# Two more matmuls with unread results in each of the first eight steps of a batch's heads

## The chip, the cores and the metric

The kernel runs on one core of one Trainium2 chip. The metric is the device time of one execution in microseconds (us). Before the change three runs took 1752.15, 1747.69 and 1748.93 us, a median of 1748.93 us.

## What is computed

The reference is a chain of four blocks over 4 sequences of 1024 tokens with 256 features, each followed by a residual and a layer norm: a gated convolution with an MLP, a mixture of 32 experts, an attention with 16 heads, and a gated MLP whose hidden values are thinned to 2 of 4. The change lies in the attention:

```python
q = (x @ w_q.T).reshape(Bc, Tc, H, D).transpose(0, 2, 1, 3)
k = (x @ w_k.T).reshape(Bc, Tc, H, D).transpose(0, 2, 1, 3)
v = (x @ w_v.T).reshape(Bc, Tc, H, D).transpose(0, 2, 1, 3)
q = _rope(q)
k = _rope(k)
scores = jnp.einsum('bhqd,bhkd->bhqk', q, k) * SCALE
scores = jnp.where(tok_mask[None, None], scores, -jnp.inf)
attn = jax.nn.softmax(scores, axis=-1)
ctx = jnp.einsum('bhqk,bhkd->bhqd', attn, v)
```

Every query sees its own and all earlier blocks of 64 keys (the mask is causal by block), and the softmax is taken over each row.

## The kernel before, in words

There are three phases (convolution and MLP; experts; attention and last MLP), each with one instruction list per engine, written out by hand: the order of a list is the order of the code, and semaphores alone tie the engines together. The third phase, `attention_ffn_phase`, takes the four sequences one after the other ("batches", b = 0 to 3). A batch has its heads first, then the output projection, the MLP and its residual; pieces of the next batch's projections are woven into the MLP.

The 16 heads of a batch are four groups (g = 0 to 3) of four heads, each two pairs. The softmax needs the maximum of every row before the exponentials, so every score is computed twice on TensorE:

- `for_maximum(b, g, m)` (L1938 and L1941) makes a piece of plain scores for maximum m of group g, 40 maxima to a group. VectorE reads the piece and reduces it (`maximum`, L1681 and L1686). The pieces go round three PSUM banks; for_maximum waits on `mx_ok` until VectorE has read the piece that lay in the bank before.
- `scores(b, g, s)` (L1965) makes the transposed scores of step s, 20 steps (`STEPS`) to a group, with the maximum already folded into q. They go into one of two double banks, `W[s % 2]`, after ScalarE's exponentials of step s - 2 have read it (`exp_ok`). ScalarE takes the exponentials (`exponentials`, L1522).
- `weighted(b, g, u, part)` (L1985), once for two steps, multiplies the weights with v, in float32, four heads beside each other in the array.
- `sums_transposed` (L1995) turns the sums back, and VectorE divides (`normalised`).

In `heads(b)` on TensorE, each step s issues the maxima due in it (`max_jobs`), then `scores` of step s + 1, then, in even steps, `weighted` of the two steps before. The maxima are made ahead: group 0's own maxima are made in the batch before (or at the phase's start), and in group 0 the first eight steps (`AHEAD` = 8) make three maxima each for group 1; all later steps make two. VectorE and ScalarE walk through the same steps.

`kept_busy(bank, count)` (L2001) exists already: it issues `count` matmuls of a 128x128 identity (float16) with 512 columns of `w_qk`, whose results nobody reads. Before the change it is called once per batch, with six matmuls, behind `scores(b, 0, 0)`, ahead of the transposes of q with its maximum (`q_max_transposed`, L1917), which ScalarE copies (L1516) before `scores(b, 0, 1)` can start.

Of the kernel before, what the change touches and what calls it, by code (L numbers as in the profile page):

```python
# [62 lines left out]
def wait(eng, sem, value):  # L63

    if not isinstance(value, int) or value > 0:
        eng.wait_ge(sem, value)  # L66
# [1053 lines left out]
LEAD = 4  # L1120
# [15 lines left out]
STEPS = 2 * NU  # L1136
AHEAD = 8
# [20 lines left out]
def attention_ffn_phase(nc, io, keep):  # L1158
    with ExitStack() as ctx:  # L1159
# [67 lines left out]
        W = S[0:2]  # L1227
# [56 lines left out]
        def group(b, g):  # L1284

            return Step(None, 0, b * NHG + g)
# [5 lines left out]
        def max_jobs(g, s):  # L1292

            if g == 0 and s < AHEAD:
                return ((1, 3 * s, 3 * s + 3),)
            low = AHEAD + 2 * s
            return ((g + 1, low, low + 2),) if low < 2 * NX else ((g + 2, low - 2 * NX, low - 2 * NX + 2),)
# [595 lines left out]
        def _(pe):  # L1893
# [20 lines left out]
            def q_max_transposed(b, pair):  # L1914
                wait(pe, nm_ok, group(b, 0)(2, LEAD + pair + 1))
                for t in range(ST):
                    last = pe.transpose(q_max_bank(pair)[:, t * P:(t + 1) * P], rows_of(0, 0, pair)[:, t * P:(t + 1) * P], ident_h[:, :])  # L1917
                last.then_inc(tm_mm, 1)

            def for_maximum(b, g, m):  # L1920
                pair, k = divmod(m, NX)
                head = 64 * (k % 2)
                q = group(b, g)
                if k == 0:
                    wait(pe, qk_in[pair], q(32, 32))
                if (g, m) == (0, 0):
                    wait(pe, qkv_ok, (b + 1) * ST)
                if g == 0:
                    wait(pe, mx_ok, q(2 * NX, LEAD + m - 1))
                else:  # L1930
                    wait(pe, *ring_bank_read(b, turns["max", g, m]))
                bank = max_bank(g, m)
                query, key = of_pair(qT, g, pair), of_pair(kT, g, pair)
                at = 0
                for i, j, count in PIECES[k // 2]:
                    plain = count - (j + count - 1 == i)
                    if plain:
                        last = pe.matmul(bank[:, at * P:(at + plain) * P], query[head:head + NORM, i * P:(i + 1) * P],  # L1938
                                         key[head:head + NORM, j * P:(j + plain) * P], start=True, stop=True)
                    if plain < count:  # L1940
                        last = pe.matmul(bank[:, (at + plain) * P:(at + count) * P],  # L1941
                                         query[head:head + USED, i * P:(i + 1) * P],
                                         key[head:head + USED, i * P:(i + 1) * P], start=True, stop=True)
                    at += count
                last.then_inc(x_mm, 1)

            def for_maxima(b, g, low, high):
                for m in range(low, high):
                    for_maximum(b, g, m)

            def scores(b, g, s):
                u, pair = divmod(s, 2)
                q = group(b, g)
                if u == 0:
                    q_max_landed(pe, b, g, pair)
                wait(pe, exp_ok, q(STEPS, LEAD + s - 1))
                query, key = of_pair(qT, g, pair), of_pair(kT, g, pair)
                at = 0
                for j, i, count in UNITS[u][1]:
                    for rows, low, high in ((USED, i, i + 1), (FILTER, i + 1, i + count)) if i == j else (  # L1960
                            (FILTER, i, i + count),):
                        if high > low:
                            for head in range(2):
                                first = 64 * head
                                last = pe.matmul(W[s % 2][:, head, (at + low - i) * P:(at + high - i) * P],  # L1965
                                                 key[first:first + rows, j * P:(j + 1) * P],
                                                 query[first:first + rows, low * P:high * P], start=True, stop=True)
                    at += count
                last.then_inc(sc_mm, 1)

            def weighted(b, g, u, part):
                half = UNITS[u][0]
                q = group(b, g)
                first = u in (0, ENDS[0] + 1)
                if part == 0:
                    wait(pe, exp_ok, q(STEPS, LEAD + 2 * u + 2))
                    if first:
                        wait(pe, ev_ok, q(2, LEAD + half))
                    if (g, u) == (0, 0):
                        wait(pe, f2_ok, 2 * b)  # L1980
                if part == len(WEIGHTED[u]):
                    return
                at, j, i, count = WEIGHTED[u][part]
                for h in range(HG):
                    last = pe.matmul(O[32 * h:32 * h + 32, (i - half * GT) * P:(i - half * GT + count) * P],  # L1985
                                     v[:, j, g * HG + h, :], weights[(g * NU + u) % SLOTS_P][:, h, at * P:(at + count) * P],
                                     start=first and part == 0, stop=u in ENDS)
                if part == len(WEIGHTED[u]) - 1:
                    last.then_inc(pv_mm, 1)

            def sums_transposed(b, g, half):
                wait(pe, ev_ok, group(b, g)(2, LEAD + half + 1))
                wait(pe, *ring_bank_read(b, turns["sum", g, half]))
                for t in range(GT):
                    last = pe.transpose(sum_bank(g, half)[:, t * P:(t + 1) * P], oT[half][:, t * P:(t + 1) * P], ident[:])  # L1995
                last.then_inc(bt_mm, 1)

            def kept_busy(bank, count):

                for i in range(count):  # L2000
                    pe.matmul(bank, ident_h[:, :], w_qk[:, 0, 0, :], start=True, stop=True)  # L2001

            def heads(b):
                scores(b, 0, 0)
                kept_busy(S[1][:, 0, :], 6)
                q_max_transposed(b, 1)
                for g in range(NHG):
                    for s in range(STEPS):
                        if s == 0 and g > 0:
                            weighted(b, g - 1, NU - 1, 0)  # L2010
                        for of, low, high in max_jobs(g, s):
                            if of < NHG:
                                for_maxima(b, of, low, high)
                        if s + 1 < STEPS:
                            scores(b, g, s + 1)
                        elif g + 1 < NHG:
                            scores(b, g + 1, 0)
                        if s == 1 and g > 0:
                            sums_transposed(b, g - 1, 1)
                        if s == 9:  # L2020
                            sums_transposed(b, g, 0)
                        if s > 0 and s % 2 == 0:
                            weighted(b, g, s // 2 - 1, 0)
                        if s > 0 and s % 2 == 0:
                            weighted(b, g, s // 2 - 1, 1)
                weighted(b, NHG - 1, NU - 1, 0)
                sums_transposed(b, NHG - 1, 1)
# [69 lines left out]
            for b in range(NB):  # L2097
# [13 lines left out]
                def at_end_of_second(t, i):  # L2111
                    if ahead and t > 0:
                        for_maximum(c, 0, 28 + 4 * (t - 1) + i)

                heads(b)
                if b == 0:
                    pe.wait_ge(consts, 16 * 5)
# [111 lines left out]
```

## Time and profile before

| | before |
|---|---|
| median of three runs | 1748.93 us |
| profiled execution, its own time | 1751.17 us |
| its span, first to last instruction | 1749.4 us |
| mean granted TensorE clock | 0.914 of full speed |
| TensorE matmul busy | 1486.2 us (85%) |
| VectorE busy | 1140.8 us (65%) |
| ScalarE busy | 732.8 us (42%) |

Busy times overlap, since the engines run beside each other. A matmul's end is modelled with its latency, so a TensorE shown as busy may still be waiting between matmuls; the granted clock is the share of full speed at which the array ran, and in a stretch of uniform clock it reads 1.00 (2.4 GHz) or 0.50 (1.2 GHz).

### The profile page before, as it was taken

The page shows a single profiled execution, that of the slowest core. Times are in us where ns is not written, and L with a number is a line of the kernel's source. Part 1 is how long each engine was busy: PE and PEld are TensorE (multiplying, and loading weights), DVE is VectorE, ACT ScalarE, POOL GpSimd, SP SyncE. Part 2 cuts the span into 40 slices and gives each one's busy share as a digit, 9 for nine tenths or more (in the row PEclk, how much of TensorE's full clock was granted, in tenths as well). Part 3 has the DMA queues.
Part 4 walks back from the last instruction along what each step waited for, and adds up shares of the span by engine and source line. Part 5 has one row for each costly group of instructions (what it writes and reads, how often), then busy time and mean ns, then how long its engine had stood idle before and what let it go on. Part 6 is the DMA issues. An engine that isn't in the chain of part 4 may idle for free.

```text
span 1749.4 us, 25732 instructions
## 1 busy us (share of the span) xinstructions
PE 1486.2 (85%) x9682; PEld 827.5 (47%) x9683; DVE 1140.8 (65%) x2275; ACT 732.8 (42%) x1232; POOL 244.8 (14%) x249
## 2 busy tenths in 40 slices
PE   4999999877989983589878988878998788988796
PEld 2666666653657873223343533253533254433355
DVE  5666666636421135678669779768779678688475
ACT  5444455512212220426744137843137752157530
POOL 3344444411410001000020000120000120000000
PEclk8999999978999977758999979998979998989999
DMA  2000001005105512222101022101022101221000
GB/s 111 13 25 25 24 26 33 24 13 180 36 24 148 157 38 105 42 37 43 31 16 34 1 43 55 37 19 31 6 38 56 43 19 25 37 34 34 31 1 25
DMA packets 137483, 75.21 MB, mean 43 GB/s; under 512 B 117648, under 2 KB 126352, under 8 KB 136592
## 3 DMA queue, kind: packets, MB, share of 16 engines
q1 hardware_dynamic: 136800, 72.02, 16.6%
q0 software_dynamic: 576, 1.77, 0.4%
q8 instruction: 67, 1.10, 0.3%
q14 instruction: 40, 0.33, 0.1%
HBM read 37.59 MB, written 9.06 MB: 27 GB/s over the span
## 4 chain that ended last, share of the span: by engine, by line
issue 58%; POOL 3%; DVE 0%; POOLq 0%; DVEq 0%
POOL xs_sb L1448 1%; POOL rs_sb L1442 1%; POOL ve_sb L1439 0%; POOL qks_sb L1462 0%; POOL v_sb L1460 0%; DVE bn_sb L1620 0%; POOL qks_sb L1452 0%; DVE x_sb_sb L1635 0%; POOLq L1159 0%; POOLq L66 0%; DVE mv_sb L1626 0%; DVEq L1159 0%; POOL v_sb L1459 0%; POOL qks_sb L1463 0%; DVE ident_h_sb L1808 0%
## 5 line engine op out<-in xcount | busy, mean ns | idle before, releaser
L1522 ACT ACTIVATE room_sb<-s_ps 128x1024 f32<-128x1024 f32 (+1 forms) x320 | 291.2, 941 | 173.7 <-PE s_ps L1965 169.8
L1686 DVE TENSOR_REDUCE mx_sb<-s_ps 128x1 f32<-128x512 f32 (+1 forms) x400 | 249.6, 650 | 73.1 <-PE s_ps L1941 46.8
L1938 PE MATMUL s_ps<-room_sb 48*128 48x512 f16 (+3 forms) x480 | 155.9, 362 | 30.2 <-DVE mx_sb L1681 17.1
L1985 PE MATMUL cm_ps<-room_sb,v_sb 128*32 128x512 f32 (+3 forms) x1536 | 171.3, 536 | 0.8 <-ACT room_sb L1528 0.8
L1965 PE MATMUL s_ps<-room_sb 51*128 51x128 f16 (+4 forms) x1152 | 154.1, 288 | 15.4 <-ACT room_sb L1522 10.6
L2080 PE MATMUL cm_ps<-w_fd_sb,room_sb 128*128 128x256 f32 x512 | 132.7, 408 | 13.3 <-DVE room_sb L1764 13.3
L1439 POOL TENSOR_TENSOR ve_sb<-mv_sb,eps_sb 128x4 f32<-128x4 f32 x24 | 5.0, 210 | 951.2 <-DVE mv_sb L1626 951.2
L396 DVE SCALAR_TENSOR_TENSOR x_sb_sb<-xp_sb,conv_w_sb,x_sb_sb 128x512 f32<-128x512 f32 x96 | 106.7, 1114 | 22.6 <-ACT x_sb_sb L319 20.5
L1938 PEld LDWEIGHTS s_ps<-room_sb 48*128 48x128 f16 x480 | 42.9, 96 | 165.3 <-DVE mx_sb L1686 84.4
L2080 PEld LDWEIGHTS cm_ps<-w_fd_sb,room_sb 128*128 128x128 f32 x512 | 98.3, 200 | 38.1 <-issue 14.1
L2067 PE MATMUL s_ps<-xbT_sb,w_fg_sb 128*128 128x512 f16 x384 | 103.3, 400 | 14.3 <-DVE ctok_sb L1734 12.7
L2067 PE MATMUL s_ps<-xbT_sb,w_fu_sb 128*128 128x512 f16 x384 | 102.9, 399 | 0.0
L966 PE MATMUL em_ps<-xT_sb,ws_gu_sb 128*128 128x512 f32 x192 | 91.1, 620 | 8.1 <-DMA rows<-zeros 8.1
L1965 PEld LDWEIGHTS s_ps<-room_sb 50*128 50x128 f16 (+1 forms) x1152 | 59.5, 98 | 66.9 <-ACT room_sb L1522 45.0
L1910 PE MATMUL s_ps<-w_qk_sb,xt_sb 128*128 128x512 f16 x192 | 52.0, 411 | 45.4 <-DMA xt_sb<-xs_sb 31.2
L1941 PE MATMUL s_ps<-room_sb 51*128 51x128 f16 x360 | 70.6, 241 | 19.7 <-DMA room_sb<-qks_sb 12.1
L1686 DVE TENSOR_REDUCE mx_sb<-cm_ps 128x1 f32<-128x512 f32 (+1 forms) x112 | 73.4, 655 | 21.3 <-PE s_ps L1941 14.0
L402 DVE SCALAR_TENSOR_TENSOR m1T_sb<-mm_ps,m1T_sb 128x512 f16<-128x512 f32 x64 | 44.0, 688 | 56.3 <-ACT m1T_sb L311 56.1
L1553 ACT ACTIVATE sgl_sb<-s_ps 128x512 f32<-128x512 f32 x64 | 37.9, 593 | 89.1 <-PE s_ps L2067 89.0
L490 PE MATMUL ro_ps<-w_dn_sb,m1T_sb 128*128 128x256 f16 x256 | 69.8, 273 | 0.8
L491 PE MATMUL ro_ps<-w_dn_sb,m1T_sb 128*128 128x256 f16 x256 | 69.8, 273 | 0.0
L492 PE MATMUL ro_ps<-w_dn_sb,m1T_sb 128*128 128x256 f16 x256 | 69.8, 273 | 0.0
(256 smaller groups left out, 2942.7 us busy)
## 6 DMA issues: line engine op xcount, KB each, us to landing
we_gu_sb<-we_gu SPq DMA_DIRECT2D x32, 352.0 KB
we_dn_sb<-we_dn SPq DMA_DIRECT2D x32, 176.0 KB
x_in_sb<-x SPq DMA_DIRECT2D x9, 512.0 KB, 3.6
rows<-x_sb_sb SPq DMA_DIRECT2D x8, 512.0 KB, 3.0
x_sb_sb<-rows SPq DMA_DIRECT2D x2, 2048.0 KB, 11.4
out<-x_sb_sb SPq DMA_DIRECT2D x8, 512.0 KB, 2.6
room_sb<-qks_sb SPq DMA_TRANSPOSE x88, 3.3
xp_sb<-w_in SPq DMA_DIRECT2D x1, 1024.0 KB, 5.6
```

The costliest lines, as they stand in the source:

```text
L396: dve.scalar_tensor_tensor(xc[:, c, :], xp[:, c, k:k + GTOK], conv_w[:, c, k:k + 1], xc[:, c, :], ALU.mult, ALU.add)\
L490: pe.matmul(out, of[0][at], by[0][cols], start=start, stop=False)
L491: pe.matmul(out, of[1][at], by[0][cols], start=False, stop=False)
L966: last = pe.matmul(mm[c % 4][:, :], ws_gu[:, k, col:col + P], xT[:, k, g * GTOK:(g + 1) * GTOK], start=(k == 0), stop=(k == KD - 1))
L1522: act.activation(weights[(g * NU + u) % SLOTS_P][:, 2 * pair:2 * pair + 2, 0:width(u) * P], W[s % 2][:, :, 0:width(u) * P], ACT.Exp, scale ...
L1686: dve.tensor_reduce(mx[:, pair, k % 2, slot:slot + 1], max_bank(g, m)[:, 0:count * P], AX.X, ALU.max, negate=True).then_inc(mx_ok, 1)
L1938: last = pe.matmul(bank[:, at * P:(at + plain) * P], query[head:head + NORM, i * P:(i + 1) * P], key[head:head + NORM, j * P:(j + plain) * ...
L1941: last = pe.matmul(bank[:, (at + plain) * P:(at + count) * P], query[head:head + USED, i * P:(i + 1) * P], key[head:head + USED, i * P:(i ...
L1965: last = pe.matmul(W[s % 2][:, head, (at + low - i) * P:(at + high - i) * P], key[first:first + rows, j * P:(j + 1) * P], query[first:firs ...
L1985: last = pe.matmul(O[32 * h:32 * h + 32, (i - half * GT) * P:(i - half * GT + count) * P], v[:, j, g * HG + h, :], weights[(g * NU + u) % ...
L2067: last = pe.matmul(bank[:, e, :], wt[:, j, k, ch * P:(ch + 1) * P], xh[:, g, k, i, :], start=(k == n == 0), stop=(k == KD - 1 and n == 2))
L2080: last = pe.matmul(CM[:, t // 2, (t % 2) * D:(t % 2 + 1) * D], hs[:, k % 3 * 4 + i, t * P:(t + 1) * P], w_fd[:, k % 2 * 4 + i, :], start=( ...
```

## The change

In steps 0 to 7 of group 0 of every batch, TensorE issues two matmuls of `kept_busy` between the step's maxima and the scores of the next step. They write the first half of the double bank into which those scores go, and a wait on the exponentials that last read it stands ahead of them.

```diff
--- before.py
+++ after.py
@@ -2011,6 +2011,9 @@
                         for of, low, high in max_jobs(g, s):
                             if of < NHG:
                                 for_maxima(b, of, low, high)
+                        if g == 0 and s < AHEAD:
+                            wait(pe, exp_ok, group(b, 0)(STEPS, LEAD + s))
+                            kept_busy(W[(s + 1) % 2][:, 0, :], 2)
                         if s + 1 < STEPS:
                             scores(b, g, s + 1)
                         elif g + 1 < NHG:
```

These are 2 x 8 x 4 = 64 matmuls more in an execution, each with its own weight load; nothing is removed.

How TensorE's list moves, at step 0 of group 0 (batch 0): L1938 and L1941 are the last pieces for maxima of the step, L2001 the added matmuls, L1965 the transposed scores of step 1.

```order
@@ -1299,4 +1299,5 @@
 L1938 MATMUL cm_ps<-room_sb 128x128
 L1941 MATMUL cm_ps<-room_sb 128x128
+L2001 MATMUL s_ps<-w_qk_sb,ident_h_sb 128x512 x2
 L1965 MATMUL s_ps<-room_sb 128x128 x2
 L1965 MATMUL s_ps<-room_sb 128x384 x2
```

The two added matmuls stand between the pieces for the maxima and the scores, and nothing else changes place.

The same list at steps 5 and 6, where a step's work is larger: L1985 is the product of weights and v that closes step 6.

```order
@@ -1336,7 +1341,9 @@
 L1938 MATMUL s_ps<-room_sb 128x512 x2
 L1938 MATMUL cm_ps<-room_sb 128x512
+L2001 MATMUL s_ps<-w_qk_sb,ident_h_sb 128x512 x2
 L1965 MATMUL s_ps<-room_sb 128x512 x2
 L1938 MATMUL s_ps<-room_sb 128x512 x2
 L1941 MATMUL cm_ps<-room_sb 128x128 x2
+L2001 MATMUL s_ps<-w_qk_sb,ident_h_sb 128x512 x2
 L1965 MATMUL s_ps<-room_sb 128x512 x2
 L1985 MATMUL cm_ps<-room_sb,v_sb 32x256 x4
```

Here too the pair comes after the step's three pieces for maxima and ahead of the scores, and the even step's product follows behind both.

## Rows read from the trace of the kernel before

**Rows 1.** The page, 40 equal slices of the span: granted TensorE clock in tenths.

```profile
PEclk8999999978999977758999979998979998989999
```

**Rows 2.** Windows of group 0: length, busy PE PEld DVE ACT POOL (count), clock, DMA, GB/s.

```profile
772.10:775.50 3.40, 2.30 (x34) 1.41 (x33) 2.64 (x6) 2.54 (x3) 0.00 (x0) 1.00 0.02 5
775.50:802.90 27.40, 27.07 (x145) 7.38 (x145) 18.18 (x36) 11.74 (x14) 0.00 (x0) 0.50 0.05 10
...
1026.30:1031.50 5.20, 4.34 (x45) 2.24 (x44) 4.99 (x11) 3.73 (x4) 0.00 (x0) 1.00 0.00 0
1031.50:1052.00 20.50, 20.04 (x116) 6.23 (x118) 14.47 (x30) 8.81 (x11) 0.00 (x0) 0.50 0.07 14
...
1281.00:1291.00 10.00, 8.14 (x82) 3.67 (x85) 9.28 (x19) 5.75 (x7) 0.00 (x0) 1.00 0.01 2
1291.00:1311.40 20.40, 20.22 (x110) 5.34 (x102) 13.61 (x28) 9.46 (x11) 0.00 (x0) 0.50 0.07 13
...
1543.50:1550.40 6.90, 5.48 (x51) 1.91 (x50) 6.72 (x12) 2.95 (x4) 0.00 (x0) 0.99 0.01 2
1550.40:1557.20 6.80, 6.36 (x41) 2.42 (x38) 4.47 (x12) 3.74 (x5) 0.00 (x0) 0.50 0.21 39
```

**Rows 3.** ACT timeline, first exponentials of groups 0 and 1, by batch: start, us, instruction, idle.

```profile
770.47 1.02 ACT L1522 ACTIVATE room_sb<-s_ps 128x1024 f32<-128x1024 f32 x1
...
810.22 1.02 ACT L1522 ACTIVATE room_sb<-s_ps 128x1024 f32<-128x1024 f32 x1 [0.90 <-PE s_ps L1965]
...
1026.42 1.02 ACT L1522 ACTIVATE room_sb<-s_ps 128x1024 f32<-128x1024 f32 x1 [15.55 <-PE s_ps L1965]
...
1063.80 1.02 ACT L1522 ACTIVATE room_sb<-s_ps 128x1024 f32<-128x1024 f32 x1 [0.90 <-PE s_ps L1965]
...
1281.08 1.02 ACT L1522 ACTIVATE room_sb<-s_ps 128x1024 f32<-128x1024 f32 x1 [15.75 <-PE s_ps L1965]
...
1318.81 1.02 ACT L1522 ACTIVATE room_sb<-s_ps 128x1024 f32<-128x1024 f32 x1 [0.90 <-PE s_ps L1965]
...
1534.63 1.02 ACT L1522 ACTIVATE room_sb<-s_ps 128x1024 f32<-128x1024 f32 x1 [15.84 <-PE s_ps L1965]
...
1569.69 1.02 ACT L1522 ACTIVATE room_sb<-s_ps 128x1024 f32<-128x1024 f32 x1 [0.90 <-PE s_ps L1965]
```

**Rows 4.** ACT timeline, steps 5 (batch 2), 5 and 7 (batch 3), 8 and 12 (batch 1).

```profile
1290.86 0.60 ACT L1522 ACTIVATE room_sb<-s_ps 128x512 f32<-128x512 f32 x1 [1.56 <-PE s_ps L1965]
...
1545.79 0.60 ACT L1522 ACTIVATE room_sb<-s_ps 128x512 f32<-128x512 f32 x1 [1.38 <-PE s_ps L1965]
...
1549.67 1.02 ACT L1522 ACTIVATE room_sb<-s_ps 128x1024 f32<-128x1024 f32 x1 [0.97 <-PE s_ps L1965]
...
1045.60 2.06 ACT L1522 ACTIVATE room_sb<-s_ps 128x1024 f32<-128x1024 f32 x2 [0.70 <-PE s_ps L1965]
...
1053.25 2.19 ACT L1522 ACTIVATE room_sb<-s_ps 128x1024 f32<-128x1024 f32 x2 [0.84 <-PE s_ps L1965]
```

**Rows 5.** PE timeline: batches 0 and 1 at the start, batches 1 and 2 in step 2.

```profile
769.04 2.74 PE L2001 MATMUL s_ps<-w_qk_sb,ident_h_sb 128*128 128x512 f16 x6
...
1026.31 1.47 PE L2001 MATMUL s_ps<-w_qk_sb,ident_h_sb 128*128 128x512 f16 x6
...
1029.39 0.39 PE L1965 MATMUL s_ps<-room_sb 51*128 51x128 f16 x4 [0.25 <-ACT room_sb L1516]
...
1032.69 1.93 PE L1985 MATMUL cm_ps<-room_sb,v_sb 128*32 128x512 f32 x8
...
1286.94 1.07 PE L1985 MATMUL cm_ps<-room_sb,v_sb 128*32 128x512 f32 x8
```

**Rows 6.** DVE timeline, maxima behind step 2's product: batch 0, batch 2; batch 3, step 6.

```profile
779.36 1.29 DVE L1686 TENSOR_REDUCE mx_sb<-s_ps 128x1 f32<-128x512 f32 x2 [2.00 <-PE s_ps L1941]
...
1288.36 1.29 DVE L1686 TENSOR_REDUCE mx_sb<-s_ps 128x1 f32<-128x512 f32 x2 [0.51 <-PE s_ps L1941]
...
1545.10 1.28 DVE L1686 TENSOR_REDUCE mx_sb<-s_ps 128x1 f32<-128x512 f32 x2
```

## The prediction, made before the change was run

> **What bounds the kernel now.** I began with the page: TensorE is busy for 85% of the span, so no other engine limits the whole, but its clock row [rows 1] has dips, and four of them lie where a batch's heads begin. Next I read that stretch in windows [rows 2]. In batch 0 the clock is at 1.00 (2.4 GHz) from 772.1 to 775.5 us and then at 0.50 (1.2 GHz) until 802.9 us; batch 1 loses it at 1031.5 for 20.5 us, batch 2 at 1291.0 for 20.4 us, batch 3 in shorter pieces. What TensorE did before each fall is the same: it ran the small pieces of the first steps, with waits on ScalarE and VectorE between them, such as the 0.25 us ahead of the scores of step 1 [rows 5].
>
> The third view is ScalarE's timeline. A group of heads begins with its first exponential, so the distance between the first exponentials of groups 0 and 1 [rows 3] is what group 0 costs: 39.75 us in batch 0 (810.22 - 770.47), 37.38 in batch 1, 37.73 in batch 2, 35.06 in batch 3, together 149.92 us. All four do the same work. The longer the clock was low, the longer the group, and batch 3, with the shortest dips, is the fastest.
>
> Last, who waits at either clock. In step 2 the product of weights and v takes 1.07 us at full clock and 1.93 at half [rows 5], and behind it VectorE idles 0.51 us in batch 2, 2.00 in batch 0 [rows 6]. At full clock two maxima take 1.28 us [rows 6], three some 1.9 us, and in batch 3's full stretch VectorE is busy 6.72 of 6.90 us [rows 2]. So at full clock VectorE's maxima set the pace of these steps; at half clock TensorE does, and VectorE is busy for only 18.18 of 27.40 us [rows 2].
>
> **What group 0 takes if the clock stays up.** No batch shows it whole, so I put it together from full-clock pieces. Steps 0 to 5: 9.78 us in batch 2 (1290.86 - 1281.08) [rows 3, 4]. Steps 5 to 7: 3.88 us in batch 3 (1549.67 - 1545.79) [rows 4]. Step 7 to 8: half of that, 1.94, an estimate. Steps 12 to 20: 10.55 us in batch 1 (1063.80 - 1053.25) [rows 3, 4], or 1.32 a step; steps 8 to 12 at that pace are 5.28, also an estimate. The sum is 31.43 us.
>
> **The change, part by part.** It removes nothing and moves nothing. It adds 64 matmuls and 32 waits.
>
> The wait costs nothing: it asks for the exponentials of the step before the current one, just what the scores behind it ask for already (both want the same double bank free). Whoever queues behind it, the scores and in even steps the product, queued behind that condition before.
>
> The matmuls: the six existing ones take 1.47 us at full clock and 2.74 at half [rows 5], so a pair takes at most 0.49 or 0.91 us, weight loads in it. On the path that is nothing where TensorE would have waited, and the whole pair where VectorE is waiting for TensorE. In step 0 the pair falls into the time in which TensorE waits for ScalarE's copy of q. In odd steps TensorE has only scores between two rounds of maxima, and VectorE has up to three banks, 1.9 us of work, in hand: nothing. In even steps the product also lies between. In step 2 VectorE idles already at full clock (the 0.51 us of [rows 6]), so the pair is paid in full; step 4 has a product of the same four tile products, and I count its pair in full too; step 6's product is half as long and I count nothing. That is 2 x 0.49 = 0.98 us a batch. The bounds are nothing at all and all eight pairs, 3.9 us; I take the lower part because VectorE is the engine at its limit in the full-clock stretch. If that cover is gone, the upper bound is the price.
>
> The clock: with pairs in every early step TensorE's waits between small pieces are filled with matmuls that use the whole array. The case for it is in the same trace: in batch 0 the clock was at half before the six existing unread matmuls and stood at 1.00 right behind them, at 772.1 [rows 2, 5]. I take it that the clock then holds through group 0, since the steps from 12 on hold it by themselves (1052.0 to 1063.8 us in batch 1 ran at full pace).
>
> The Trainium skill, "TensorE: Matmul & The Clock Gate", section "HAM oscillation — how this bites in real kernels", speaks against this: it puts the loss of the clock down to long idle waits of the engine between tiles, and by it steps whose waits are as short as these would not lose it for want of work, so unread matmuls would give nothing. The trace disagrees, since batch 1 loses the clock at 1031.5 with a wait of 0.25 us in the stretch ahead; the page's next section, on short pauses between groups of matmuls, fits better.
>
> **The sum.** Group 0 with the change: 31.43 + 0.98 = 32.41 us, four times 129.64. Against 149.92 that is 20.3 us less: 7.3 in batch 0, 5.0, 5.3 and 2.7 in the others. Nothing behind group 0 takes this back, as I see it: the last eight steps of group 0 already ran at full clock in batch 1, so the transposing DMAs and waits of later groups meet the same pace as there. The profiled execution took 1751.17 us, which gives 1730.9; it stands 2.2 us above the median of the runs, from which the same gain gives 1728.6. I predict 1730. With the pairs costing nothing the gain is 24 us (1726); a dip less in a later group may add some us. This case's own range is 1723 to 1739.
>
> **The rivals.**
>
> *The clock holds, but every pair lands on the path*, because TensorE, which takes its list in order, becomes the pace of these steps. 31.43 + 3.9 = 35.3 us a group, gain 8.7 us: 1741. For it: VectorE idles behind step 2's product even at full clock [rows 6]. Against: VectorE 97% busy in the full stretch [rows 2].
>
> *The clock holds while there are pairs and falls when they end at step 8.* Steps 8 to 12 took 7.65 us in batch 1 at half clock (1053.25 - 1045.60) [rows 4] against the 5.28 above, so 2.4 us come back; batch 0, which stayed low longer, was 2.4 us longer still, so up to 4.8. Four times that is 9.5 to 19 us: 1740 to 1750. For it: the dips of before do reach beyond step 8. Against: they began before it.
>
> *Slower: the clock falls in the first stretch all the same*, behind the copy of q, because two matmuls a step are too few there. Then the six pairs of steps 2 to 7 run at half clock, where TensorE is the pace, and each costs 0.91 us: 5.5 us a batch, 22 in all, 1771. The point that decides is the granted clock some 5 us after a batch's first exponential. For it: six unread matmuls already stand just ahead, and batch 1 falls 3.7 us after they end (1031.50 against 1027.78). Against: at half clock the pairs leave so little waiting that the clock should come back early, as it did in batch 0 behind the six.
>
> *The fall has a cause that matmuls don't touch*, as the skill's rule on idle waits would have it. The place and price are as in the case before, 1771.
>
> **How the numbers follow.** Chances: forecast 0.66, every pair on the path 0.13, fall at step 8 0.09, fall in the first stretch 0.08, another cause 0.04. A measurement of this kernel can tell about 0.3%, 5.2 us, from no change; the bound for faster is 1743.7. Faster: the first two and a little of the third, less something for mixtures, 0.78. Same: most of the third, and mixtures of batches that hold and batches that don't, 0.10. Slower: the last two, 0.12. The range of 1722 to 1746 takes in the forecast's own range, the second case and half of the third.
>
> **What would show it.** Right: the windows of group 0 at clock 1.00 from a batch's first exponential to its 20th step, the distance between first exponentials of groups 0 and 1 near 32.4 us in all four batches, VectorE's idle time behind the product of step 2 up to about 1.0 us and hardly any in odd steps, the new matmuls some 0.22 to 0.25 us apart. The prediction is wrong if one of these windows stands at 0.50 for long, if the groups are alike but 35 us or more, or if group 0 shrinks and a later stage grows by as much.

## The result, and the profile after

The changed kernel's median is 1732.06 us in seven runs (1730.14 to 1741.10), the kernel before stands at 1748.18 us in the seven beside them (1740.49 to 1752.29). The ratio is 0.9912, 95% interval 0.9892 to 0.9933: faster by about 0.9%, some 16 us. The prediction was 1730 us, in a range of 1722 to 1746.

| | before | after |
|---|---|---|
| profiled execution, its own time | 1751.17 us | 1732.06 us |
| span | 1749.4 us | 1730.2 us |
| mean granted TensorE clock | 0.914 | 0.937 |
| group 0, batches 0 to 3 | 39.75, 37.38, 37.73, 35.06 us | 33.60, 33.51, 33.50, 33.50 us |

The page's clock row after, in 40 slices, against [rows 1]:

```profile
PEclk8999999987999987759999999988999999999999
```

The dips of before at the heads of batches 1 to 3 (the single 7s and 8s at 1006, 1268 and 1531 us) are gone. The 8, 7, 7, 5 that stay in the middle belong to the stage ahead of the heads of batch 0, which begin at 768 us. The windows of group 0, with the columns of [rows 2]:

```profile
767.90:772.10 4.20, 4.15 (x34) 2.16 (x31) 1.61 (x4) 2.53 (x3) 0.00 (x0) 0.72 0.00 0
772.10:799.50 27.40, 24.92 (x222) 8.39 (x220) 24.12 (x49) 16.84 (x19) 0.00 (x0) 1.00 0.06 12
...
1014.30:1047.80 33.50, 30.73 (x290) 11.26 (x293) 29.50 (x60) 20.10 (x22) 0.00 (x0) 1.00 0.10 19
1266.30:1299.80 33.50, 30.74 (x290) 11.27 (x294) 29.51 (x60) 20.10 (x22) 0.00 (x0) 1.00 0.10 18
1518.10:1551.60 33.50, 30.73 (x290) 11.27 (x294) 29.51 (x60) 20.10 (x22) 0.00 (x0) 1.00 0.10 18
```

The clock is 1.00 (2.4 GHz) throughout in batches 1 to 3, and in batch 0 but for a piece of its first 4.2 us, whose mean is 0.72. Before, batch 0 spent 27.4 us of this group at 0.50, batches 1 and 2 some 20 us each [rows 2]. VectorE is now busy 29.5 of 33.5 us, 88%; in the half-clock stretch of batch 0 before it was 18.18 of 27.40, 66% [rows 2]. The first exponentials of groups 0 and 1 in ScalarE's timeline, against [rows 3]:

```profile
767.90 1.02 ACT L1522 ACTIVATE room_sb<-s_ps 128x1024 f32<-128x1024 f32 x1
...
801.50 1.02 ACT L1522 ACTIVATE room_sb<-s_ps 128x1024 f32<-128x1024 f32 x1 [0.90 <-PE s_ps L1965]
...
1014.31 1.02 ACT L1522 ACTIVATE room_sb<-s_ps 128x1024 f32<-128x1024 f32 x1 [15.61 <-PE s_ps L1965]
...
1047.82 1.02 ACT L1522 ACTIVATE room_sb<-s_ps 128x1024 f32<-128x1024 f32 x1 [0.90 <-PE s_ps L1965]
```

All four batches now take the same time, 33.5 us, which is what a group at a steady clock should do. Summed over the batches group 0 shrank from 149.92 to 134.11 us, by 15.8 us. The profiled execution's own time shrank by 19.1 us; from the first exponential of group 0 to the last of group 3 the four batches together gained 17.0 us (in batch 3 a dip in group 1 went as well), and the other 2 us lie in stages that the change doesn't touch. Even ahead of batch 0's heads, where no added matmul has run yet, this execution is 2.6 us earlier than the one before (767.90 against 770.47 [rows 3]); so single executions differ by some us with the same code up to there.

What the pairs cost is read from TensorE's and VectorE's timelines in batch 1, against [rows 5] and [rows 6]. TensorE after, the scores of step 1 and then step 2:

```profile
1017.51 0.40 PE L1965 MATMUL s_ps<-room_sb 51*128 51x128 f16 x4
...
1019.85 0.33 PE L1938 MATMUL cm_ps<-room_sb 48*128 48x384 f16 x1
1020.02 0.22 PE L1941 MATMUL cm_ps<-room_sb 51*128 51x128 f16 x1
1020.17 0.61 PE L2001 MATMUL s_ps<-w_qk_sb,ident_h_sb 128*128 128x512 f16 x2
1020.71 0.40 PE L1965 MATMUL s_ps<-room_sb 51*128 51x128 f16 x6
1021.04 1.07 PE L1985 MATMUL cm_ps<-room_sb,v_sb 128*32 128x512 f32 x8
1022.04 0.34 PE L1938 MATMUL s_ps<-room_sb 48*128 48x384 f16 x2
```

The same step in batch 2 of the kernel before, which had the clock at 1.00 there:

```profile
1286.40 0.34 PE L1965 MATMUL s_ps<-room_sb 51*128 51x128 f16 x2
1286.56 0.22 PE L1941 MATMUL cm_ps<-room_sb 51*128 51x128 f16 x1
1286.58 0.43 PE L1965 MATMUL s_ps<-room_sb 51*128 51x128 f16 x4
1286.94 1.07 PE L1985 MATMUL cm_ps<-room_sb,v_sb 128*32 128x512 f32 x8
```

Before, the first scores began beside the last piece for a maximum (1286.40 against 1286.56). Now they begin 0.69 us behind it (1020.71 - 1020.02): 0.15 us pass ahead of the pair, and the pair itself holds them back for 0.54 us. The product of weights and v begins 1.02 us behind the last piece (1021.04 - 1020.02) and not 0.38 (1286.94 - 1286.56), so 0.64 us later. VectorE's waits in group 0 of the same batch after:

```profile
1018.17 0.69 DVE L1681 TENSOR_REDUCE mx_sb<-s_ps 128x2 f32<-128x512 f32 x1 [0.33 <-PE s_ps L1941]
...
1022.47 1.29 DVE L1686 TENSOR_REDUCE mx_sb<-s_ps 128x1 f32<-128x512 f32 x2 [1.15 <-PE s_ps L1941]
...
1026.91 1.29 DVE L1686 TENSOR_REDUCE mx_sb<-s_ps 128x1 f32<-128x512 f32 x2 [0.77 <-PE s_ps L1938]
```

It waits 1.15 us behind step 2's product, against 0.51 at full clock and 2.00 at half before [rows 6], so again 0.64 us more at full clock; 0.77 us behind step 4's; 0.33 us in step 1, where the scores now begin 3.20 us behind the batch's first exponential (1017.51 - 1014.31) and not 2.97 (1029.39 - 1026.42 [rows 3, 5]): step 0's pair outlasts the wait for ScalarE's copy by 0.2 us.

### The profile page after: what moved, and what is told of

It reads as the page before. It is cut to its first block, busy times and chain, and to the rows that moved or that the text cites. A ratio compares the mean times of both kernels' runs of the same rounds, so it can differ in the third digit from the quotient of the medians.

```text
span 1730.2 us, 25860 instructions
## 1 busy us (share of the span) xinstructions
PE 1467.9 (85%) x9746; PEld 824.5 (48%) x9747; DVE 1141.1 (66%) x2275; ACT 732.3 (42%) x1232; POOL 244.5 (14%) x249
## 4 chain that ended last, share of the span: by engine, by line
issue 58%; POOL 3%; DVE 0%; POOLq 0%; DVEq 0%
POOL xs_sb L1448 1%; POOL rs_sb L1442 1%; POOL ve_sb L1439 0%; POOL qks_sb L1462 0%; POOL v_sb L1460 0%; DVE bn_sb L1620 0%; POOL qks_sb L1452 0%; DVE x_sb_sb L1635 0%; POOLq L1159 0%; POOLq L66 0%; DVE mv_sb L1626 0%; DVEq L1159 0%; POOL v_sb L1459 0%; POOL qks_sb L1463 0%; DVE ident_h_sb L1808 0%
## 5 line engine op out<-in xcount | busy, mean ns | idle before, releaser
L1938 PE MATMUL s_ps<-room_sb 48*128 48x512 f16 (+3 forms) x480 | 145.2, 340 | 31.7 <-DVE mx_sb L1681 19.2
L1985 PE MATMUL cm_ps<-room_sb,v_sb 128*32 128x512 f32 (+3 forms) x1536 | 156.8, 496 | 0.8 <-ACT room_sb L1528 0.8
L1965 PE MATMUL s_ps<-room_sb 51*128 51x128 f16 (+4 forms) x1152 | 137.2, 274 | 14.1 <-ACT room_sb L1522 10.6
L1938 PEld LDWEIGHTS s_ps<-room_sb 48*128 48x128 f16 x480 | 41.7, 94 | 151.8 <-DVE mx_sb L1686 80.7
L1965 PEld LDWEIGHTS s_ps<-room_sb 50*128 50x128 f16 (+1 forms) x1152 | 53.5, 95 | 74.5 <-ACT room_sb L1522 46.5
L1941 PE MATMUL s_ps<-room_sb 51*128 51x128 f16 x360 | 65.5, 229 | 18.6 <-DMA room_sb<-qks_sb 11.0
```

## The experiments

Theory A is the prediction's: unread matmuls in TensorE's waits keep its clock at 1.00, and the gain is that clock. The rivals are put in each expectation. Lines that a diff doesn't show stand as in the change. In what follows "group 0" is the distance between the first exponentials of groups 0 and 1, in ScalarE's timeline, for batches 0 to 3 in this order.

**The waits without the matmuls.**

```diff
-                            kept_busy(W[(s + 1) % 2][:, 0, :], 2)
```

> The eight added waits a batch, without the matmuls. Theory A (the unread matmuls hold TensorE's clock): nothing holds it, so group 0 takes 35 to 40 us again with the clock at half from about step 3 on; the waits cost under 1 us in all; about 1748 us. Rival B (the gain comes from the order, the scores held back behind the wait, and not from the clock): group 0 takes 33.5 us as with the change, about 1732 us.

The ratio to the kernel before is 0.9992 (0.9978 to 1.0006), 1745.55 us beside 1745.98. Group 0 took 37.56, 34.00, 37.42 and 35.05 us, and the windows show the clock gone again:

```profile
777.10:797.60 20.50, 20.13 (x116) 6.50 (x120) 14.46 (x30) 8.81 (x11) 0.00 (x0) 0.50 0.08 14
1036.60:1046.80 10.20, 10.02 (x64) 2.98 (x56) 7.54 (x17) 4.76 (x6) 0.00 (x0) 0.50 0.14 27
1285.70:1306.20 20.50, 20.05 (x116) 6.45 (x118) 14.47 (x30) 8.82 (x11) 0.00 (x0) 0.50 0.07 14
```

Rival B falls: the order and the waits give nothing and cost nothing that can be told in the total. Group 0 took 144.0 us together in this profile, against 149.9 in that of the kernel before, mostly because batch 1 lost the clock later and for 10.2 us only (34.00 against 37.38 us). So the 15.8 us above are the difference of two single profiles, and how much group 0 loses in a typical execution of the kernel before is not shown.

**One matmul a step in place of two.**

```diff
-                            kept_busy(W[(s + 1) % 2][:, 0, :], 2)
+                            kept_busy(W[(s + 1) % 2][:, 0, :], 1)
```

> One unread matmul a step in place of two. Theory A: if one is enough for the clock, group 0 loses about 0.2 us in each step in which the pair lay on the path, some 1 us a batch: 32.5 us, about 1728 us in all. If one is too little, the clock falls in the first steps in some batches and group 0 takes 35 to 38 us there: 1738 to 1745 us. Rival B has no use for the number of matmuls: 1728 us whatever the clock.

0.9965 (0.9944 to 0.9985), 1741.18 us. Group 0: 35.27, 36.02, 32.68, 34.97 us. One profile holds both cases:

```profile
1026.10:1036.30 10.20, 10.10 (x55) 2.55 (x55) 5.37 (x11) 2.64 (x4) 0.00 (x0) 0.50 0.00 0
1275.60:1308.30 32.70, 29.48 (x282) 11.14 (x284) 29.41 (x60) 20.18 (x23) 0.00 (x0) 1.00 0.10 20
```

Batch 2 kept the clock and took 32.7 us; batch 1 lost it for 10.2 us and took 36.0. Instructions and order are the same in both, so the 3.3 us between them are the clock. One a step is not enough here, and it is cheaper by 0.8 us where the clock does hold (32.7 against 33.5).

**Which steps need the pair.** Three runs: the pair in steps 0 to 2 alone, in steps 0, 1, 3, 5 and 7 alone, and in steps 3 to 7 alone.

```diff
-                        if g == 0 and s < AHEAD:
+                        if g == 0 and s < 3:
```

> Pairs in steps 0 to 2 alone. Theory A, every early step needs them: the fall is only put off, as in batch 2 of the kernel before, which kept its clock for the first 10 us and lost it then; group 0 takes 36 to 38 us, about 1744 us. Rival C, only the first stretch is at risk: the clock holds, five pairs are saved, group 0 takes 32.2 to 33 us, about 1728 us.

```diff
-                        if g == 0 and s < AHEAD:
+                        if g == 0 and s in (0, 1, 3, 5, 7):
```

> Pairs in steps 0, 1, 3, 5 and 7 alone, where no product of weights and v follows them. If the price of the change is paid in the even steps (VectorE idles 1.15 us behind step 2's product and 0.77 behind step 4's with the change), group 0 falls from 33.5 to about 32.3 us while the clock holds: about 1727 us. If the clock needs the pairs of the even steps too, some batches lose it after step 3: 35 to 38 us there, 1738 to 1745 us.

```diff
-                        if g == 0 and s < AHEAD:
+                        if g == 0 and 3 <= s < AHEAD:
```

> Pairs in steps 3 to 7 alone, none in steps 0 to 2. Theory A, the first steps need them too: the clock falls within some 8 us of the first exponential in two to four batches, as before the change; the pairs of steps 3 to 7 then run at half clock at 0.9 us each until it comes back, group 0 34 to 38 us there, 1738 to 1748 us. Rival C, in the form that only the later steps are at risk: the clock holds in all four, group 0 32.5 to 33 us, about 1730 us.

Steps 0 to 2 alone: group 0 took 33.94, 34.60, 34.02 and 36.00 us, and every batch held the clock for some 15 to 17 us and then lost it. The fall is put off, as expected, but the time is shorter than I had expected: the half-clock stretches in group 0 last 3.4 to 10.2 us. The total is no better than before all the same: 1750.31 us, ratio 1.0025 (1.0002 to 1.0048). In its profile the stages outside the heads took 1319 us of the span against 1313 in the kernel before; but that profile is of an execution of 1745.41 us, some 5 us below the median, so where the median lost the gain of group 0 is not shown. I come back to these stages below. Batch 2 of this run also shows steps 5 to 8 without pairs at full clock, which is used further down (its first exponential stands at 1275.17 us):

```profile
1275.20:1292.30 17.10, 14.24 (x134) 5.72 (x133) 15.28 (x32) 9.21 (x11) 0.00 (x0) 1.00 0.02 3
```

```profile
1285.81 0.60 ACT L1522 ACTIVATE room_sb<-s_ps 128x512 f32<-128x512 f32 x1 [1.56 <-PE s_ps L1965]
...
1289.69 1.02 ACT L1522 ACTIVATE room_sb<-s_ps 128x1024 f32<-128x1024 f32 x1 [0.97 <-PE s_ps L1965]
...
1291.91 1.02 ACT L1522 ACTIVATE room_sb<-s_ps 128x1024 f32<-128x1024 f32 x1 [0.71 <-PE s_ps L1965]
```

The first is its window with the clock at 1.00, the others are the exponentials of steps 5, 7 and 8.

Steps 0, 1, 3, 5 and 7: 0.9947 (0.9925 to 0.9968), 1739.38 us; group 0 34.72, 34.87, 32.20, 33.74 us. Batch 2 kept the clock, and its 32.20 us is what the group takes without pairs in the even steps 2, 4 and 6. The others lost it some 15 us behind the first exponential, for 3.4 to 6.8 us; this run's windows:

```profile
1035.80:1042.60 6.80, 6.78 (x34) 2.23 (x36) 3.65 (x8) 2.96 (x3) 0.00 (x0) 0.50 0.21 40
1274.70:1306.90 32.20, 29.00 (x284) 11.02 (x288) 29.48 (x60) 20.10 (x22) 0.00 (x0) 1.00 0.10 19
```

Steps 3 to 7 alone (one execution, 1734.68 us beside 1740.33 of the kernel before): group 0 32.26, 32.64, 35.77, 33.82 us. Batches 0 and 1 kept the clock without pairs in the first steps, batches 2 and 3 lost it from 1270.5 us for 10.2 us and from 1526.5 us for 3.4 us:

```profile
1015.10:1047.60 32.50, 29.15 (x284) 10.91 (x286) 29.38 (x60) 19.89 (x22) 0.00 (x0) 1.00 0.10 19
1270.50:1280.70 10.20, 10.20 (x55) 2.20 (x51) 6.00 (x11) 2.22 (x3) 0.00 (x0) 0.50 0.01 2
```

So neither half of the steps holds it in every batch: early steps without pairs lose it in some batches, late steps in others. Rival C falls in both forms.

**Steps 2 and 4 without the pair.** VectorE waits behind the products of steps 2 and 4; of the pairs left out in the run with steps 0, 1, 3, 5 and 7, step 6's was taken for the one that the clock missed.

```diff
-                        if g == 0 and s < AHEAD:
+                        if g == 0 and s in (0, 1, 3, 5, 6, 7):
```

> Pairs in steps 0, 1, 3, 5, 6 and 7: the run with 0, 1, 3, 5 and 7 lost its clock some 15 us after the first exponential in three batches of four, about when step 6 ends, and took 32.2 us in the one that held it. Theory A: with step 6's pair back the clock holds in all four batches, and only step 6's pair is paid for, if anything: group 0 takes 32.2 to 32.6 us, about 4 us less than the change in all, 1727 to 1729 us. Rival D (steps 2 and 4 are needed too): clock falls in some batches, group 0 34 to 35 us there, 1735 to 1740 us.

This version was then measured a second time, beside the change itself; the two expectations are these, the change's first.

> The change once more, beside the next run on the same chip: clock at 1.00 through group 0, 33.5 us each, 1730 to 1737 us.

> Pairs in steps 0, 1, 3, 5, 6 and 7 once more, beside the change: group 0 took 32.2 us against 33.5, so some 5 us less than the change in all if nothing else differs. If what the clock does in other stages outweighs that, no difference that can be told.

Group 0 took 32.13, 32.21, 32.21 and 32.22 us, and in the second run 32.11, 32.21, 32.20 and 32.21: the clock holds in all eight, and 1.3 us a batch are saved against the change. The 32.2 us are also what batch 2 took above without step 6's pair, so that pair adds nothing beside those of steps 5 and 7. Its windows in the second run:

```profile
1016.80:1049.00 32.20, 29.51 (x290) 11.04 (x288) 29.48 (x60) 20.11 (x23) 0.00 (x0) 1.00 0.11 21
1270.70:1302.90 32.20, 29.53 (x290) 11.05 (x288) 29.49 (x60) 20.11 (x23) 0.00 (x0) 1.00 0.11 21
1522.80:1555.00 32.20, 29.52 (x290) 11.01 (x288) 29.48 (x60) 20.11 (x23) 0.00 (x0) 1.00 0.11 21
```

In all it is not faster than the change: 1734.07 us (0.9922, 0.9899 to 0.9946), then 1736.59 (0.9935, 0.9912 to 0.9958) beside the change's 1736.32 (0.9938, 0.9915 to 0.9961) on the same chip. The 5 us of the expectation are given back behind group 0: in the second run's profile 2.5 us of them in dips of the clock in groups 1 and 2, and the rest and more outside the heads. The stages from the heads of one batch to those of the next, in the change's profile:

```profile
872.80:1014.30 141.50, 122.78 (x593) 66.83 (x586) 107.98 (x181) 44.28 (x90) 11.69 (x14) 0.95 0.14 27
1119.10:1266.30 147.20, 126.95 (x593) 68.97 (x586) 108.89 (x187) 44.34 (x90) 12.22 (x15) 0.92 0.14 26
1371.30:1518.10 146.80, 126.04 (x593) 68.39 (x586) 108.92 (x187) 44.34 (x90) 12.22 (x15) 0.93 0.14 26
```

And in the second run without steps 2 and 4:

```profile
872.40:1016.70 144.30, 127.25 (x589) 66.99 (x582) 108.19 (x181) 44.50 (x90) 11.55 (x14) 0.92 0.14 26
1121.40:1270.60 149.20, 127.61 (x592) 70.36 (x582) 108.75 (x187) 44.14 (x91) 12.22 (x15) 0.92 0.13 25
1374.10:1522.70 148.60, 128.12 (x592) 69.94 (x582) 108.97 (x187) 44.37 (x91) 12.23 (x15) 0.91 0.13 25
```

The code of these stages is the same, they took 442.1 us against 435.5, and the mean clock was lower in two of the three. The other profile of each version gives nearly the same, 442.2 us for this version and 437.0 for the change. The length of group 0 alone doesn't decide it: the same stages took 443.0 us in the run below on fewer columns, whose group 0 is as long as the change's, and 443.3 us with four matmuls a step, whose group 0 is longer. What does decide it is not shown.

**What a pair costs where the clock is up anyway.** The change, and the pairs in group 1 too; then four matmuls a step in group 0.

```diff
-                        if g == 0 and s < AHEAD:
-                            wait(pe, exp_ok, group(b, 0)(STEPS, LEAD + s))
+                        if g < 2 and s < AHEAD:
+                            wait(pe, exp_ok, group(b, g)(STEPS, LEAD + s))
```

> The change, and pairs in the first eight steps of group 1 too, where the clock is at 1.00 already: the bare price of a pair. Group 1 takes 26.96 us with the change. If a pair is paid for where TensorE is the later engine only, some four pairs of eight at 0.5 us are paid, 29 us; if every pair is paid, 8 x 0.6 us, 31.5 us; if pairs are free, 27 us. In all the change's 1732 us plus four times that, 1740 to 1750 us.

Group 1 took 28.55, 28.55, 28.58 and 28.55 us against 26.96: eight pairs cost 1.6 us, 0.2 us a pair, at a clock of 1.00. The first exponentials of groups 1 and 2 of batch 0 in this run:

```profile
802.87 1.02 ACT L1522 ACTIVATE room_sb<-s_ps 128x1024 f32<-128x1024 f32 x1 [0.90 <-PE s_ps L1965]
...
831.41 1.02 ACT L1522 ACTIVATE room_sb<-s_ps 128x1024 f32<-128x1024 f32 x1 [0.90 <-PE s_ps L1965]
```

In all 1743.42 us beside 1748.40, 0.9995 (0.9970 to 1.0020): by the ratio the change's gain is gone, more than four times 1.6 us account for. In its profile (1746.66 us, 14.6 more than the change's) 6.4 us are these pairs, 2.6 us are dips in group 2 of two batches, and 5.7 us lie outside the heads.

```diff
-                            kept_busy(W[(s + 1) % 2][:, 0, :], 2)
+                            kept_busy(W[(s + 1) % 2][:, 0, :], 4)
```

> Four matmuls a step in place of two, clock held either way: the slope of the price. The pairs cost 2.1 us a batch (33.5 against 31.4 put together from rows without them). If by then TensorE is the later engine in all eight steps, another pair adds 8 x 0.43 = 3.4 us: 36.9 us a group. If VectorE still hides half, 35.2 us. If the price had been the wait and its issue and not the matmuls, 33.5 us.

One execution, 1745.88 us beside a median of 1748.79; group 0 35.35, 35.29, 35.29, 35.28 us at a clock of 1.00 in batches 1 to 3. Sixteen more matmuls add 1.8 us. One matmul more takes some 0.22 us (six took 1.47 us [rows 5], two take 0.60 above), so sixteen would take 3.5 us: about half of their time is hidden, the middle case.

**The same matmuls on fewer columns.** They take as long and stand at the same places, but use 32 of the array's 128 columns.

```diff
-                            kept_busy(W[(s + 1) % 2][:, 0, :], 2)
+                            for i in range(2):
+                                pe.matmul(W[(s + 1) % 2][0:32, 0, :], ident_h[:, 0:32], w_qk[:, 0, 0, :], start=True, stop=True)
```

> The change with the same 64 matmuls, of the same length and at the same places, but on 32 of the 128 columns of the array. Theory A in the form that any running matmul counts: as the change, clock at 1.00 through group 0, 33.5 us each, about 1732 us. Rival E (what counts is how much of the array works): the clock falls in group 0 of most batches, 36 to 40 us each with the pairs paid for at half clock, 1745 to 1755 us.

0.9947 (0.9924 to 0.9969), 1738.03 us; group 0 34.07, 33.49, 33.49, 33.50 us:

```profile
1020.90:1054.30 33.40, 30.62 (x290) 11.26 (x292) 29.42 (x60) 20.01 (x23) 0.00 (x0) 1.00 0.10 19
1275.10:1308.60 33.50, 30.72 (x290) 11.28 (x292) 29.52 (x60) 20.11 (x23) 0.00 (x0) 1.00 0.10 19
```

The clock is 1.00 here too, and rival E falls for this case. Batch 0 takes 0.5 us more than with the change; it leaves the half clock of the stage before later, at 771.8 us, 3.8 us behind its first exponential.

**Without the six at the start.** This is the run without steps 2 and 4, and without the six unread matmuls that the kernel had already.

```diff
-                kept_busy(S[1][:, 0, :], 6)
```

> The run with pairs in steps 0, 1, 3, 5, 6 and 7, without the six unread matmuls at a batch's start. If the six are still needed, the clock falls within 5 us of the first exponential in most batches, or never rises in batch 0: 35 us or more there. If the pairs hold it alone, each group 0 is shorter by up to the six's 1.3 us, 31 to 32.2 us, and batch 0, which starts at half clock, is the one at risk.

Group 0 took 34.42, 34.30, 34.28 and 34.25 us, 2.1 us more than with the six. In batch 0 the clock stays at half until 780.6 us, 12.7 us behind the first exponential (the first line), and in batches 1 to 3 it falls right behind the first exponential:

```profile
767.90:780.60 12.70, 12.70 (x84) 4.79 (x85) 8.22 (x15) 6.16 (x7) 0.00 (x0) 0.50 0.00 1
1016.20:1023.00 6.80, 6.67 (x50) 2.74 (x48) 4.99 (x10) 3.86 (x4) 0.00 (x0) 0.51 0.01 2
1265.30:1272.10 6.80, 6.67 (x47) 2.82 (x50) 5.03 (x10) 3.78 (x4) 0.00 (x0) 0.50 0.01 4
1517.90:1524.70 6.80, 6.69 (x48) 2.86 (x50) 5.03 (x10) 3.71 (x4) 0.00 (x0) 0.50 0.00 0
```

The six and the pairs do one work between them, each for its own stretch. The total, 1730.77 us (0.9915, 0.9881 to 0.9948), is among the lowest, though the heads of all batches together took 7 us longer than with the six (423 us against 416, from the first exponential of group 0 to the last of group 3); so what it gains elsewhere comes from the stages outside the heads, which took 1307 us in this profile. No version that I ran beats the change by more than can be measured.

## Why the prediction was right, point by point

**What bounds group 0.** Right in the main. At a steady 1.00 VectorE is busy 29.5 of 33.5 us and waits for the rest, and all batches take the same time. The full-clock time of the group, put at 31.43 us, comes out at 31.35 from stretches without pairs: steps 0 to 5 the 9.78 us of the prediction, steps 5 to 8 6.10 us in the run with pairs in steps 0 to 2 alone (1291.91 - 1285.81), steps 8 to 20 15.47 us in batch 1 after (1047.82 - 1032.35). That the sum fits so well is luck: both of its estimates were off, step 7 to 8 takes 2.22 us (1291.91 - 1289.69) and not 1.94, steps 8 to 20 take 15.47 and not 15.83, and the errors cancel.

**The wait costs nothing.** Shown by the run with the waits alone, as far as a total can tell (0.9978 to 1.0006 of the kernel before).

**The clock holds.** Shown, and as a cause: one matmul a step held it in one batch and not in the others, and the same code then took 32.7 or 35 to 36 us.

**The price of the pairs** is the term that was mis-sized. I took 0.98 us a batch, for steps 2 and 4 alone; it is 33.5 - 31.35 = 2.15 us. The exponentials of steps 5 and 8 in batch 1 after:

```profile
1025.60 0.60 ACT L1522 ACTIVATE room_sb<-s_ps 128x512 f32<-128x512 f32 x1 [1.55 <-PE s_ps L1965]
...
1032.35 2.90 ACT L1522 ACTIVATE room_sb<-s_ps 128x1024 f32<-128x1024 f32 x3 [0.72 <-PE s_ps L1965]
```

| pair in step | predicted | measured | from |
|---|---|---|---|
| 0 | 0 | 0.23 us | scores of step 1, 3.20 us behind the first exponential against 2.97 |
| 2 and 4 | 0.49 us each | 1.3 us together | 33.5 us against 32.2 without the two |
| 1, 3 | 0 | 0 | see below |
| 5 to 7 | 0 | 0.65 us together | 6.75 us from step 5 to step 8 (1032.35 - 1025.60) against 6.10 |

Steps 2 and 4 cost 0.64 to 0.65 us each because a pair sets the product back by 0.64 us, the 0.15 us ahead of it included, and not by 0.49. Step 0's pair outlasts the wait it was to fill. The pairs of steps 1 and 3 are free: with them, and none in steps 2 and 4, step 5 begins 0.2 us later than before, which is step 0's share. Of steps 5 to 7, step 6's pair adds nothing, as predicted, but the 0.65 us are paid with the pairs of steps 5 and 7 alone: without step 6's, batch 2 took 6.75 us there too (1291.47 - 1284.72). For these two odd steps together the prediction's "nothing" did not hold.

**The sum.** Predicted 20.3 us, measured 15.8 in group 0 and about 16 in the median; the 4.5 us between them are, to 0.2 us, four times the 1.2 us by which the price was put too low. Measured a second time the change's median was 12.5 us below (1736.32 against 1748.79), with the same 33.5 us a group. Of the 19.1 us that the profiled execution lost, 3.3 us are a dip in another group and stages that were not touched; that they bring it closer to the forecast is luck.

**The rivals.** Every pair on the path (3.9 us a batch) was the nearest: about half of it came true. The fall at step 8 did not happen with eight pairs; with pairs in steps 0 to 2 alone the clock fell some 15 to 17 us behind the first exponential, about step 8, five steps behind the last pair. The slower case, a fall in the first stretch, did not come with two a step, and came with one a step and with none of the six. The Trainium skill, "TensorE: Matmul & The Clock Gate", section "HAM oscillation — how this bites in real kernels", puts the loss of the clock down to long idle waits of the engine. That does not describe this kernel: in group 0 of the kernel before, TensorE's longest wait ahead of a fall was 0.67 us (batch 0, ahead of the scores at 773.55 us), and the clock stayed up when matmuls were put into the early steps.

**Nothing behind group 0 takes it back.** For the change this held within 2 us. It is no law: the version that saved 1.3 us a batch more lost it in stages that have the same code.

## What to carry to other kernels

Where the same work takes different times in different iterations, look at the granted clock by stretch before anything else; the iteration with the clock up is the measure of what there is to gain. Filling short waits of TensorE with matmuls whose results nobody reads can pay for itself, if another engine sets the pace at full clock, and the filler is cheapest in the steps where that engine has work in hand; too little filler held the clock in some batches only (one a step, 0.35% in all) or gained nothing (steps 0 to 2 alone). Judge such an edit by the stage's own time in the profile as well as by the total, since the clock in untouched stages moves the total by several us.

## What was not expected of the hardware

Matmuls on 32 of the 128 columns kept the granted clock at 1.00 as the full ones did, group 0 33.5 us with either.

A stage with unchanged code, from the heads of batch 0 to those of batch 1, took 141.5 us in the change's profile, at a mean clock of 0.95, and 144.3 us in another version's, at 0.92. Over all stages outside the heads the profiles differ from 1307 to 1322 us. The heads of batch 0, ahead of which all versions run the same code, begin between 764.4 and 772.3 us. What decides where the clock falls there stays open; it wasn't tried to hold it.
